# Recurrent attention and mixture-of-experts block: the weighted sum of the first layer issued one unit later

## The reference

```python
xn = layernorm(x)
s  = attention0(xn)      # two attentions of 8 heads (width 8), one on a Holt-smoothed copy; o-projection, layernorm, FFN
g  = silu(top1_of_16_experts(xn))
x  = x + s * g
xn = layernorm(x)
s  = attention1(xn)      # 16 heads (width 8), causal, ALiBi
g  = silu(top2_of_8_experts(xn))
x  = x + s * g
```

## Time and profile before

| | |
|---|---|
| median of 3 runs | 1276.57 us (1275.53 to 1281.41) |
| the profiled execution's own time | 1285.47 us |
| its span | 1283.5 us |
| TensorE busy | 1049.2 us, 82% of the span |
| TensorE weight load | 544.6 us, 42% |
| VectorE busy | 776.5 us, 60% |
| ScalarE busy | 656.6 us, 51% |
| GpSimd busy | 541.2 us, 42% |
| DMA | 137.60 MB, mean 107 GB/s |
| granted TensorE clock, mean | 0.926 of full speed |

### The profile page before, as it was taken

How to read it: one execution, slowest core, us unless ns; L and a number is a source line. 1 busy time by engine, 2 the same in 40 slices (tenths; PEclk the granted TensorE clock), 3 DMA queues, 4 the chain that set the end, 5 groups by cost and what they waited for, 6 DMA issues and landing times.

```text
span 1283.5 us, 24573 instructions
## 1 busy us (share of the span) xinstructions
PE 1049.2 (82%) x8630; PEld 544.6 (42%) x8630; DVE 776.5 (60%) x1696; ACT 656.6 (51%) x1245; POOL 541.2 (42%) x568
## 2 busy tenths in 40 slices
PE   5349889969989898988899787784699978889982
PEld 5112249623333333333334444342589944434541
DVE  6359772457878787878755646754244446557710
ACT  1000662446767666667666545353244446556672
POOL 3154400062727272737363724477100056654344
PEclk9955999989999999999999989797799989899997
DMA  6345347661414141414141415244488843433211
GB/s 180 118 124 127 85 131 211 209 148 34 105 29 106 29 103 34 108 26 116 27 117 27 117 26 151 68 123 136 115 243 249 239 121 89 111 82 87 60 35 41
DMA packets 133348, 137.60 MB, mean 107 GB/s; under 512 B 14233, under 2 KB 115193, under 8 KB 133017
## 3 DMA queue, kind: packets, MB, share of 16 engines
q1 hardware_dynamic: 127096, 123.59, 37.1%
q0 software_dynamic: 6144, 12.60, 3.8%
HBM read 88.11 MB, written 54.58 MB: 111 GB/s over the span
## 4 chain that ended last, share of the span: by engine, by line
PE 51%; POOL 18%; DVE 9%; issue 6%; ACT 6%; DMA 4%; SPq 1%; POOLq 0%; ACTq 0%; DVEq 0%
PE ps_banks L526 7%; PE ps_banks L491 5%; PE ps_banks L1422 5%; PE ps_banks L483 5%; POOL sent L1552 5%; POOL tokens L868 4%; DVE a_neg_max L727 4%; PE ps_banks L602 3%; PE ps_banks L1435 2%; PE ps_banks L1217 2%; PE ps_banks L1203 2%; PE ps_banks L597 2%; PE ps_banks L545 2%; PE ps_banks L502 2%; PE ps_banks L566 2%
## 5 line engine op out<-in xcount | busy, mean ns | idle before, releaser
L727 DVE TENSOR_REDUCE a_neg_max<-ps_banks 128x1 f32<-128x512 f32 x512 | 325.8, 684 | 95.2 <-PE ps_banks L491 93.3
L642 ACT ACTIVATE a_probs<-ps_banks 128x512 f32<-128x512 f32 x512 | 282.9, 598 | 142.8 <-PE ps_banks L483 140.5
L491 PE MATMUL ps_banks<-k_strip,q_strip 51*128 51x128 bf16 (+2 forms) x1536 | 299.0, 296 | 42.9 <-DMA k_strip<-k_rows 21.6
L483 PE MATMUL ps_banks<-q_strip,k_strip 53*128 53x128 bf16 (+3 forms) x1408 | 283.7, 299 | 16.8 <-DVE a_neg_max L727 6.8
L644 ACT ACTIVATE a_probs<-ps_banks 128x512 f32<-128x512 f32 x256 | 146.9, 598 | 113.6 <-PE ps_banks L483 111.0
L491 PEld LDWEIGHTS ps_banks<-k_strip,q_strip 51*128 51x128 bf16 x1536 | 101.3, 95 | 233.9 <-ACT a_probs L642 109.7
L868 POOL DMA_INDIRECT tokens<-made,at x96 | 92.9, 968 | 155.5 <-DMA made<-work 127.9
L483 PEld LDWEIGHTS ps_banks<-q_strip,k_strip 53*128 53x128 bf16 x1408 | 94.8, 95 | 123.2 <-ACT a_probs L642 52.6
L729 DVE TENSOR_REDUCE a_neg_block<-ps_banks 128x4 f32<-128x512 f32 x128 | 87.2, 689 | 95.9 <-PE ps_banks L491 94.7
L526 PE MATMUL ps_banks<-a_probs,v_aug 128*32 128x512 f32 x1024 | 140.4, 621 | 0.0
L732 DVE TENSOR_REDUCE a_neg_block<-ps_banks 128x4 f32<-128x512 f32 x128 | 83.2, 683 | 31.8 <-PE ps_banks L491 31.5
(11 more groups left out here) (223 smaller groups left out, 1691.1 us busy)
## 6 DMA issues: line engine op xcount, KB each, us to landing
work<-in_pack SPq DMA_DIRECT2D x40, 450.0 KB, 3.5
q_rows<-a_q_parts SPq DMA_DIRECT2D x96, 128.0 KB
k_rows<-a_k_parts SPq DMA_DIRECT2D x96, 128.0 KB
q_strip<-q_rows SPq DMA_DIRECT2D x64, 192.0 KB
k_strip<-k_rows SPq DMA_DIRECT2D x64, 192.0 KB
work<-in_w SPq DMA_DIRECT2D x32, 256.0 KB, 3.2
sent<-in_zeros SPq DMA_DIRECT2D x14, 512.0 KB, 7.9
work<-sent SPq DMA_DIRECT2D x56, 128.0 KB, 3.2
```

The costliest lines, as they stand in the source:

```text
L483: mm = pe.matmul(sbank[:, at:at + hi - lo], k_now[rows(js, ROW_END), slot, kt * P:(kt + 1) * P], q_now[rows(js, ROW_END), slot, lo:hi], st ...
L491: mm = pe.matmul(mbank[:, at:at + hi - lo], q_next[rows(jm, ROW_SHIFT), slot, qt * P:(qt + 1) * P], k_next[rows(jm, ROW_SHIFT), slot, lo:h ...
L642: act.activation(probs[si // 4 % 2][:, si % 4, :], bank, ACT.Exp).then_inc(sems["probs"], 1)
L727: dve.tensor_reduce(neg_max[:, half, hd, qt:qt + 1], bank, AX.X, ALU.max, negate=True).then_inc(sems["max_out"], 1)
```

## The change

In the first layer the sum of group g is issued behind unit 4g+7 in place of 4g+6: a distance of QT = 4 units in place of RING = 3, and the wait in front of it (L518) allows four exponentials outstanding in place of three. The `take` of a quad follows one unit later too (behind unit 16q+20 in place of 16q+19). An odd place 2g+3 stands behind the same unit 4g+7, so the sum now stands right in front of that place's step, where it has one. The second layer keeps its distance of three. In batch 8, whose units are those of the second layer while the last sum, take and norm are those of the first, the table `LAST0` puts that `norm` at place 4 in place of 2 and `onT` at 6 in place of 5, so that they stay behind the `take`. No instruction is added or left out.

```diff
--- before.py
+++ after.py
@@ -131,6 +131,7 @@
 QUADS = H // 4
 UNITS = (H * QT, 10 * QUADS)
 PLACES = 32
+LATE = (QT, 3)
 BANKS, RING, MAX_BANK, SUM_BANK, MISC_BANK = 8, 3, 3, 6, 7
 
 MISC = {
@@ -144,6 +145,8 @@
         8: [("v", 1), ("load", 3)], 12: [("norm", 0, 0)], 16: [("fetch", 2, 0)], 17: [("proj", -1)], 19: [("shift", 1, 0)], 20: [("norm", 0, 1)],
         28: [("norm", 0, 2)]},
 }
+
+LAST0 = {**MISC[0], 2: [], 4: [("norm", -1, QT - 1)], 5: [], 6: [("onT", -1)]}
 
 EXTRA = {
     ROUTE1: {12: [("choose", 0)], 14: [("count", 0)], 15: [("send", 0, 0)], 20: [("weigh", 0)]},
@@ -216,7 +219,7 @@
 
     def misc(place):
         for k in range(2):
-            for step in MISC[k].get(place, []):
+            for step in (LAST0 if b == NB and k == 0 else MISC[k]).get(place, []):
                 if live(step[1]) and layer(step[1]) == k:
                     if step[0] == "fetch":
                         fetch(*step[1:])
@@ -239,9 +242,9 @@
     late = {}
     if live(-1):
         last = UNITS[layer(-1)]
-        late = {at + RING - last: (-1, g) for at, g in sums_of(layer(-1)).items() if at + RING >= last}
+        late = {at + LATE[layer(-1)] - last: (-1, g) for at, g in sums_of(layer(-1)).items() if at + LATE[layer(-1)] >= last}
     if live(0):
-        late.update({at + RING: (0, g) for at, g in sums_of(layer(0)).items()})
+        late.update({at + LATE[layer(0)]: (0, g) for at, g in sums_of(layer(0)).items()})
     if live(1):
         fetch(1, 1)
     if live(-1) and layer(-1) == 0:
@@ -262,7 +265,7 @@
         if mi is not None and (mi + 1) % (maxima // 2) == 0:
             add("minus", 1, mi // (maxima // 2))
         if scores and u in late:
-            total(*late[u], RING)
+            total(*late[u], LATE[layer(late[u][0])])
         while place < PLACES and (place + 1) * units <= (u + 1) * PLACES:
             misc(place)
             place += 1
```

## The result

The changed kernel takes 1303.24 us (median of 4, 1302.88 to 1304.55), the kernel before 1278.99 beside it: a ratio of 1.0192, 95% interval 1.0159 to 1.0226, or +24.3 us. The forecast was +10.5 us, within 1270 to 1294: the right way, but less than half of what was measured.

A forecast was written before the change was run, and what follows sets the result against it. TensorE, GpSimd, TensorE, then VectorE bound each batch in turn. Costs less savings gave +1.6 us a batch, 11.5 in batches 1 to 7, +0.5 batch 0, -1.5 batch 8: +10.5, 1287 us median; range 1270 to 1294.

The forecast's parts named there:

- place 10: `norm` in GpSimd's stretch: new wait at most 0.9, nearer 0.4, covered by slack and three seams: 0 (bounds 0 and 0.2).
- batch 8: Last first-layer `norm`, moved by `LAST0`: meets a finished take, `shift` and `q` no longer behind it: -1.5 us (-2.5 to +0.5).
- the end of a batch: VectorE's stretch, place 26 and unit 63: 0.9 + 0.37, less 0.68 of savings: +0.6 us a batch.
- Step (3): Take at a quad's end, later on ScalarE, delays `norm`: 0.9 at place 2, 0.87 at 18, 0 at 10, 0.9 at 26.
- seam: TensorE changeover between unit and whole-array step: one 0.32 becomes 0.23, saving 0.1 at seven odd places, 0.7 us a batch.
- rival D: Sum in front of a whole-array step needs no changeover: 0.14 more saved at seven places, 1280 us; chance 0.04.
- step (2): ScalarE free sooner at odd places: copy of `shift` 0.28 sooner, also at place 21, `onT` 0.12: 0.7 us a batch saved.
- step (4): End of VectorE's stretch: unit 63 waits for its maximum, no longer covered by the sum: 1.55 becomes 1.92, +0.37 a batch.
- Place 26: `norm` in VectorE's stretch: take later, VectorE idles and resumes 0.9 later; cost 0.9 a batch (bounds 0 and 1.0).
- rival A: VectorE's stretch has more slack, so step (4) and place 26 cost nothing: +0.37 a batch, 1278 us; chance 0.27.
- rival B: Take stays off the path at `norm`, places 2, 18, 26: -1.0 a batch, 1268 us; chance 0.10.
- Rival C: Longer idle brings more or longer drops of TensorE's clock, 0.75 each: 2 to 5 us on top, about 1291; chance 0.13.

The follow-up runs named there:

- experiment without group 3: Changed kernel with only group 3's sum and its take put back behind unit 18: 1296.34 us, 1.0134 to the kernel before; changed kernel beside it 1303.33.
- pair of one chip: Kernel before and changed kernel, both unaltered, profiled again on one chip: spans 1275.2 and 1300.0 us, 24.8 apart.
- take later: Kernel before with all sums left alone, only the first layer's take one unit later, and the change's batch 8 table: 1.0114, repeated 1.0102.
- kernel before (again): The unchanged kernel run against itself and profiled again on the chip of the changed kernel's second profile: 0.9983, span 1275.2 us.

## Why the prediction was wrong

It was 13.8 us short. One step put at zero, place 10, makes half of that, some 7 us; batch 8 makes 2.6, the end of a batch 1, and some 3 lie behind the first layer and stay open. Most other steps came out to a tenth.

**Right: the mechanism and its size at places 2 and 18.** Step (3) forecast 0.9 and 0.87 less a seam of 0.1; the table has 0.90 and 0.77.

**Right: the changeovers.** Sum to whole-array fp32 step takes 1.00, as the prediction had it from the earlier trace rows, so rival D is out. The Trainium skill (TensorEngine Tiling, Key Properties) has every change of the tiling mode drain TensorE; the trace agrees at these steps, with one changeover saved and the other kept. `shift` starts 0.89 behind its sum, which saves 0.1 more. It differs from the others in type (bf16) and in width (16 columns of the array), and which of the two matters was not tried. Of step (2) the `shift` part came (0.25 for 0.28) and the `onT` part did not: `onT` to `k` stayed 1.35, since the copy, although started earlier, took 0.61 in the chain for 0.51. Together place 2 to `proj` is 0.6 shorter, as forecast, but partly by luck: the 0.1 in front of `shift` and 0.06 at place 7, neither of them in the sum, made up for `onT`.

**Wrong: place 10 at zero.** The prediction put `proj` to `yT` down as covered: "the 0.5 of slack in front of `yT` and three seams cover it". It priced the take there at 0.4, and that was right. It did not see unit 19, so the failed step is this zero. The sum of group 3 used to stand between units 18 and 19, and VectorE, busy with the row statistics behind `proj`, had not freed unit 19's bank. From the kernel before:

```profile
463.05 1.16 PE L587 MATMUL ps_banks<-wo,a_o_T 128*128 128x128 f32 x8
...
466.40 1.07 PE L526 MATMUL ps_banks<-a_probs,v_aug 128*32 128x512 f32 x8
467.48 0.37 PE L491 MATMUL ps_banks<-k_strip,q_strip 51*128 51x512 bf16 x1
```

Unit 19 starts as far behind `proj` after as before: 4.43 us (467.48 - 463.05) and 4.44 (474.08 - 469.64). Before, the sum filled that wait and unit 19 seemed to wait for nothing. After, TensorE idles 1.01 and the sum comes behind. `x2T` is 1.0 later, `norm` 1.4 (1.0 + 0.4), `yT` 1.5, less 0.5 of slack: +0.98 a batch, 6 to 7 us over the batches. The three seams that were to help there gave nothing: apart from the slack, `norm` to `yT` takes 8.6 us before and 8.7 after. I had found this very mechanism at unit 51, step (3), and at unit 63, step (4), and not asked for it at each of the other sums. The experiment without group 3 gives 7.0 us back. Either delay alone would have met the 0.5 of slack; what one costs without the other was not tried on this chip.

**Half right: the end of a batch.** Place 26 and unit 63 were put at 0.9 + 0.37, less 0.68 of savings: +0.6. Unit 63 came out to the hundredth: the unit behind the sum starts 1.92 behind unit 62, where it was 1.55. The table's 29.46 to 29.43 looks as if the whole cost nothing. But the batch of 64.70 us that had no clock drop before carried another delay: VectorE's `mix` operation (L783) took 1.47 us there for 0.68 in the two batches ahead of it, and from its start to the next `zT` it is 7.12 us there and 6.34 in those two. Without that 0.79 the stretch would be 28.67 (an estimate), and the change costs 0.75. The rival A, which had this stretch cost nothing, is out, and rival B too.

**Wrong in size: a drop of the clock.** Rival C priced it at 0.75 by a comparison with exactly that batch. Corrected by the 0.79, a drop costs 1.3 to 1.5 (30.00 and 30.20, less 28.67) before. After, a drop is twice as long and costs 2.4 (31.86 on average against 29.43). From batch 1 to 7 they are fewer: four before, three after in the pair of one chip, so their total is 5 to 6 us before and 7 after. The difference is about the 1.9 that a faster `mix` gives back in three of these batches. The first profile of after had four. Clock and `mix` together shift single batches by 2 us and the sum by little.

**Wrong: batch 8.** Forecast -1.5 us from the table LAST0; `proj` comes 23.3 us behind the last `norm` of batch 7, where it came 23.0, and the batch is 1.1 us longer. The take's wait of 1.27 is gone from place 2, but `norm` is two places further back and the chain through it, `onT` and `proj` starts as late.

The account for the pair on one chip: 1.66 forecast a batch, + 0.98 for place 10, + 0.16 at the batch's end (0.75 for 0.59) = 2.8; measured 2.86 (from place 26 of batch 1 to that of batch 7, 392.36 and 409.53 us). That they agree this closely is luck in part, since it needs clock and `mix` to cancel. Seven such batches are 20 of the 24.8 us. Batch 8 adds 1. Some 3 us behind it, in the second layer, the change does not explain; their cause stays open, and they are of the size by which executions of one kernel differ.

## What to carry to other kernels

Work moved away from between two waiting steps can be paid twice: what waited for it waits longer, and what it was covering comes to light. A timeline without idle in front of an instruction does not say that it has no wait: for every instruction that loses its neighbour, look up when its own inputs and buffers became free, at each of its repetitions and not only where the page shows idle. And before a copy is moved in an in-order queue, count what gets ahead of it: one more exponential of 0.5 us in front of the take, and behind the odd place's copy, cost far more here than every saved changeover.

## What the runs showed of the hardware

In batches 1 to 7 the granted clock fell for 3.4 us at a time before and for 6.8 after. One such drop in each, from the pair of one chip (busy us and records of TensorE, its weight load, VectorE, ScalarE and GpSimd, then clock, DMA share, GB/s):

```profile
370.60:374.00 3.40, 3.40 (x18) 0.59 (x16) 1.99 (x6) 1.18 (x3) 3.24 (x5) 0.51 0.02 5
```

```profile
373.40:380.20 6.80, 6.00 (x32) 1.37 (x26) 3.66 (x7) 2.67 (x6) 5.43 (x6) 0.54 0.01 2
```

In front of each TensorE waits for VectorE behind `ff2`: 1.0 us before, 2.0 after (509.15 above), since the sum of group 11 no longer lies in that wait. Batches without a drop have the same waits, so a wait of this size doesn't bring a drop by itself. Nor does a long drop need the 2.0: in take later, where the wait is 1.0 as before and one of 0.6 for the take follows it, the granted clock is 0.50 over 6.8 us too (386.6 to 393.4 in the second run). What makes the drop longer stays open.

VectorE's `mix` operation reads two tensors in SBUF. In batch 4 of the kernel before (again) it started beside a GpSimd operation that had begun at 504.59, and took 1.47 us:

```profile
504.95 1.47 DVE L783 SCALAR_TENSOR_TENSOR tokens<-tokens 128x512 f32<-128x512 f32 x1
```

```profile
504.59 1.28 POOL L854 TENSOR_TENSOR work<-work,be_ff 128x512 f32<-128x512 f32 x1
```

In the changed kernel it starts 1.31 us behind GpSimd's start in place of 0.36, as GpSimd's ends, and takes 0.68:

```profile
448.27 0.68 DVE L786 SCALAR_TENSOR_TENSOR tokens<-tokens 128x512 f32<-128x512 f32 x1
```

```profile
446.96 1.26 POOL L857 TENSOR_TENSOR work<-work,be_ff 128x512 f32<-128x512 f32 x1
```

The Trainium skill (SBUF — State Buffer, Who interferes with whom) has VectorE instructions with two SBUF inputs contend with a GpSimd instruction that reads SBUF, the one that holds the shared port going through first. The trace agrees: GpSimd's operation ends at 505.87 and `mix` at 506.42, 0.55 behind it, so nearly all of `mix` ran after it. In this way a stall that delayed VectorE gave back 0.8 us of itself here.
